# Turning the last weight in the first aggregation, and degree sums by way of VectorE, in a three-layer graph network on one core

## What is computed

```
deg     = segment_sum(1, dst);  deg_inv = 1 / max(deg, 1)
h       = relu(x @ W_self0 + (segment_sum(x[src], dst) * deg_inv) @ W_neigh0 + b0)
l0      =      h @ W_self1 + (segment_sum(h[src], dst) * deg_inv) @ W_neigh1 + b1
y       = layernorm(x + l0)
rows, cols = (src, dst) with every node's loop added
s       = (count of rows) ** -0.5
l1      = segment_sum(s[rows] * s[cols] * (y @ W.T + b)[cols], rows)
out     = layernorm(y + l1)
```

## Time and profile before

| | |
|---|---|
| median of three runs | 849.19 us |
| profiled execution | 849.59 us, span 847.9 |
| TensorE busy | 830.6 us |
| VectorE, ScalarE, POOL busy | 461.3, 177.4, 459.1 us |
| DMA | 180.52 MB, mean 213 GB/s |
| granted clock | 0.999 |

### The profile page before, as it was taken

One profiled execution on the slowest core, in us unless ns is written; L12 is line 12 of the kernel. 1 busy time (PEld: TensorE's weight loads), 2 busy tenths in 40 slices (PEclk: granted clock), 3 DMA queues, 4 the chain that ended last, 5 costly groups with the idle time before them and its releaser, 6 DMA issues.

```text
span 847.9 us, 11000 instructions
## 1 busy us (share of the span) xinstructions
PE 830.6 (98%) x4295; PEld 707.9 (83%) x4295; DVE 461.3 (54%) x714; ACT 177.4 (21%) x218; POOL 459.1 (54%) x343
## 2 busy tenths in 40 slices
PE   8999999999999999999999999999999999999996
PEld 6888888888897899788888888778889889988885
DVE  6465568200017565897544677775556435455555
ACT  4111132110111113353123112222222122200000
POOL 5028887787777887885888788788620000000000
PEclk9999999999999999999999999999999999999999
DMA  9977965463776425668876668267877649555551
GB/s 332 380 304 267 350 193 168 125 176 75 213 236 180 122 57 133 249 237 286 298 282 222 243 220 284 62 176 214 240 245 255 223 150 295 189 199 199 198 193 46
DMA packets 99480, 180.52 MB, mean 213 GB/s; under 512 B 15474, under 2 KB 75898, under 8 KB 94048
## 3 DMA queue, kind: packets, MB, share of 16 engines
q1 hardware_dynamic: 60144, 124.17, 44.0%
q10 hardware_dynamic: 26896, 40.65, 13.3%
q0 software_dynamic: 12384, 14.95, 7.6%
HBM read 107.08 MB, written 72.43 MB: 212 GB/s over the span
## 4 chain that ended last, share of the span: by engine, by line
PE 61%; POOL 15%; DMA 9%; issue 8%; DVE 5%; SPq 1%; ACT 1%; POOLq 0%; ACTq 0%; DVEq 0%
PE ps L1572 19%; POOL adj_in L643 14%; PE ps L1429 12%; PE ps L1606 10%; PE ps L1589 9%; PE ps L1515 8%; DMA adj_in<-u 4%; DMA first_rows<-in_L_gnn_W_neigh 1%; DMA spare<-in_x 1%; DMA xin<-s0t_scr 1%; PE ps L1413 1%; DVE u L914 1%; PE ps L1380 1%; SPq L514 1%; DVE sacc L1303 0%
## 5 line engine op out<-in xcount | busy, mean ns | idle before, releaser
L643 POOL DMA_INDIRECT adj_out<-loops,idx_out x160 | 245.2, 1533 | 65.4 <-issue 65.4
L643 POOL DMA_INDIRECT adj_in<-mult,idx_in x160 | 198.1, 1238 | 86.8 <-issue 86.8
L1572 PE MATMUL ps<-u 128*128 128x512 f32 x840 | 190.7, 389 | 1.4 <-DVE u L914 1.4
L1572 PEld LDWEIGHTS ps<-u 128*128 128x128 f32 x840 | 157.6, 188 | 34.2 <-issue 1.6
L1484 PE MATMUL ps<-wx 128*128 128x512 f32 (+1 forms) x576 | 109.4, 351 | 1.3 <-ACT outb L761 1.3
L1484 PEld LDWEIGHTS ps<-wx 128*128 128x128 f32 x576 | 93.9, 189 | 16.9 <-ACT outb L761 1.9
L1429 PE MATMUL ps<-u 128*128 128x512 f32 x432 | 98.2, 389 | 0.0
L1515 PE MATMUL ps<-wx,u 128*128 128x256 f32 (+5 forms) x640 | 94.8, 309 | 1.2 <-DVE ht L1191 1.2
L1589 PE MATMUL ps<-u,panel_tiles 128*128 128x512 f32 (+1 forms) x400 | 93.9, 393 | 1.9 <-DVE u L914 1.9
L1429 PEld LDWEIGHTS ps<-u 128*128 128x128 f32 x432 | 81.0, 188 | 16.8
L1515 PEld LDWEIGHTS ps<-wx,u 128*128 128x128 f32 (+1 forms) x640 | 86.6, 191 | 8.2 <-DVE ht L1191 1.6
(11 more groups left out here) (167 smaller groups left out, 779.8 us busy)
## 6 DMA issues: line engine op xcount, KB each, us to landing
left_scr<-u SPq DMA_DIRECT2D x7, 2560.0 KB, 9.5
u<-left_scr SPq DMA_DIRECT2D x7, 2560.0 KB, 9.6
xt_scr<-wx ACTq DMA_DIRECT2D x10, 1024.0 KB, 9.9
u<-xt_scr SPq DMA_DIRECT2D x10, 1024.0 KB, 5.1
wx<-xt_scr SPq DMA_DIRECT2D x16, 512.0 KB, 4.0
adj_in<-u POOLq DMA_DIRECT2D x4, 1600.0 KB, 25.3
adj_out<-u POOLq DMA_DIRECT2D x4, 1600.0 KB, 16.1
wx<-adj_in SPq DMA_DIRECT2D x5, 1280.0 KB, 7.1
```

Source lines behind the costliest of these rows:

```text
L643: pool.indirect_dma_start(table, bass.IndirectOffsetOnAxis(ap=index[0:EP, j:j + 1], axis=0), counts[0:EP, j:j + 1], None, bounds_check=CEL ...
L1572: ins = nc.tensor.matmul(ps[:, product_bank(g, i, p), :], left_op[n % 2][:, p, k, left, :], right_op[n % 2][:, k, right, :], start=(not on ...
```

## The change

The turning of the GCN weight moves from the second aggregation to the first: eight turns, behind blocks 3, 8, 12, 14, 17, 20, 23 and 26, each with its load (SP, ahead of the fetches of blocks 7, 12, 16, 18, 21, 24 and 27; the first at the end of stage 2) and its copy and store (ScalarE, behind the Relus of blocks 0, 5, 8, 10, 13, 16, 19 and 23). The degrees of chunks 0 and 1 are one matmul each with column sums made by VectorE, placed behind block 0 and behind block 11 (chunk 1, d=3). The one-column matmuls go; the reciprocals go through DRAM (`dinv_scr`) and come back as a column. The self parts of blocks 0 to 3 are fetched inside stage 2. The self stage has eight staging places. Some semaphores are merged.

```diff
+    TURN_BEHIND = {3: 0, 8: 1, 12: 2, 14: 3, 17: 4, 20: 5, 23: 6, 26: 7}
+    TURN_LOADS = {7: 1, 12: 2, 16: 3, 18: 4, 21: 5, 24: 6, 27: 7}
+    TURN_COPIES = {0: 0, 5: 1, 8: 2, 10: 3, 13: 4, 16: 5, 19: 6, 23: 7}
...
-        staged = [quarter(outb[:, :, :], j) for j in range(4)]
+        staged = [quarter(buf, j) for buf in (outb[:, :, :], raw[:, :, :]) for j in range(4)]
...
+            def fetch_self(m):
+                c, d = H_BLOCKS[m]
+                for i in [S0_BLOCKS.index((b, d)) for b in {0: (0,), 1: (0, 1), 2: (1,), 3: (2,)}[c]]:
+                    sp.wait_ge(s0_stored[i % 8], 16 * (i // 8 + 1))
+                if m >= 4:
+                    sp.wait_ge(h_sum, fetch_free(m))
+                sp.dma_start(fetch_slot(m)[:, 0:CHUNKS[c][1] * T], s0t_scr[d, :, lines(CHUNKS[c])]).then_inc(s0_in[m % 8], 16)
...
+                if i == 20:
+                    sp.wait_ge(xt_turned, NT)
+                    for m in range(4):
+                        fetch_self(m)
                 if i == 21:
                     load_chunk_1(0)
+            def load_turn(k):
+                if k == 0:
+                    sp.wait_ge(s0_full, 3 * KD)
+                else:
+                    sp.wait_ge(wt_turned, k)
+                sp.dma_start(turn_in[:, :], w_gcn[k * P:(k + 1) * P, :]).then_inc(wt_in, 16)
+
+            load_turn(0)
             sp.wait_ge(m1_full[0], 16)
             load_chunk_1(1)
...
             for m, (c, d) in enumerate(H_BLOCKS):
+                if m in TURN_LOADS:
+                    load_turn(TURN_LOADS[m])
                 if m >= 4:
+                    fetch_self(m)
                 if m in (15, 23):
                     load_chunk_1(2 + m // 17)
+                if d == 6:
+                    t0, n = CHUNKS[c]
+                    sp.wait_ge(dinv_row_done, c + 1)
+                    sp.dma_start(dinv_scr[lines(CHUNKS[c])].rearrange("(a j) -> a j", a=1), dinv_row[0:1, c % 2, 0:n * T]
+                                 ).then_inc(dinv_stored[c % 2], 16)
...
+            for s in range(2):
+                sp.wait_ge(dinv_stored[s], 16 * 2)
+            sp.dma_start(dinv[:, :], dinv_scr.rearrange("(t p) -> p t", p=P), allow_slow_non_contiguous=True).then_inc(dinv_in, 16)
...
+            def keep_turned(k):
+                act.wait_ge(wt_turned, k + 1)
+                if k > 0:
+                    act.wait_ge(wt_stored, 16 * k)
+                nc.scalar.activation(turn_out[:, :], pair_bank(3), ACT.Copy).then_inc(wt_copied, 1)
+                act.wait_ge(wt_copied, k + 1)
+                act.dma_start(wt_scr.rearrange("(k p) o -> p k o", p=P)[:, :, k * P:(k + 1) * P],
+                              turn_out.rearrange("p (k o) -> p k o", k=KD)).then_inc(wt_stored, 16)
...
                 if d == 0:
+                    if c < 2:
+                        dve.wait_ge(m1_full[c], 16 * n // 2)
+                        nc.vector.tensor_reduce(sacc[:, 0:width].rearrange("p (n j) -> p n j", n=n // 2),
+                                                m1_panels[c][:, :, :, :].bitcast(F32).rearrange("p k n j -> p n j k"), AX_X, ALU.add
+                                                ).then_inc(colsum_done, 1)
+                        dve.wait_ge(colsum_done, 2 * c + 1)
+                        nc.vector.tensor_copy(colsum[:, 0:width], sacc[:, 0:width]).then_inc(colsum_done, 1)
                     dve.wait_ge(deg_full, c + 1)
...
-                if d == 5:
-                    dve.wait_ge(dcol_full, c + 1)
-                    nc.vector.tensor_copy(dinv[:, t0:t0 + n], ps[:, 6 + c % 2, 0:n]).then_inc(dcol_read, 1)
...
+            def turn_weights(row, c):
+                pe.wait_ge(wt_in, 16 * (row + 1))
+                pe.wait_ge(deg_read, c + 1)
+                if row > 0:
+                    pe.wait_ge(wt_copied, row)
                 for k in range(KD):
+                    ins = nc.tensor.transpose(pair_bank(3)[:, k * P:(k + 1) * P], turn_in[:, k * P:(k + 1) * P], ident[:, :])
                 ins.then_inc(wt_turned, 1)
...
+            def degrees(c, width, exact):
+                pe.wait_ge(s0_free, s0_bank_free(6 + c))
+                if c == 1:
+                    pe.wait_ge(wt_copied, 2)
+                pe.wait_ge(colsum_done, 2 * c + 2)
...
+                    ins = nc.tensor.matmul(bank, ones_r[:, :], colsum[:, 0:width], start=True, stop=True)
+                ins.then_inc(deg_full, 1)
...
+                    if c >= 2:
+                        pe.wait_ge(deg_read, c - 1)
+                        pe.wait_ge(wt_copied, {2: 4, 3: 7}[c])
+                        for k in range(NT):
...
-                        if d == 2:
-                            pe.wait_ge(dinv_row_done, c + 1)
-                            for i in range(n):
-                                ins = nc.tensor.matmul(ps[:, 6 + c % 2, i:i + 1], dinv_row[0:1, c % 2, i * T:(i + 1) * T],
-                                                       ones_nt[0:1, 0:1], start=True, stop=True)
-                            ins.then_inc(dcol_full, 1)
+                        if (c, d) in ((0, 0), (1, 3)):
+                            degrees(c, width, exact)
+                        if m in TURN_BEHIND:
+                            turn_weights(TURN_BEHIND[m], 0 if m == 8 else c)
...
-                        if 1 <= t <= KD:
-                            turn_weights(t - 1)
```

More of the change, by code:

```diff
@@ L92, in build @@
         base = -(-nc.sbuf_base // 32) * 32
-        U_AT, WX_AT, R_AT, E_AT, END = (base + n for n in (0, 81920, 163840, 188416, 197120))
+        U_AT, WX_AT, R_AT, E_AT, B_AT, END = (base + n for n in (0, 81920, 163840, 188416, 197120, 201216))
         sb("arena", [P, (END - base) // 4], F32)
@@ L117, in build @@
         ones_r = sb("ones_r", [P, P], F32R)
-        bias = sb("bias", [P, D], F32)
+        bias = at("bias", [P, D], F32, B_AT)
+        colsum = at("colsum", [P, WIDE], F32R, B_AT)
         ident = sb("ident", [P, P], F32)
@@ L280, in build @@
         res_full = sems("res_full", 2)
-        wt_in = sems("wt_in", 2)
-        wt_stored = sems("wt_stored", 2)
+        wt_in = sem("wt_in")
+        wt_stored = sem("wt_stored")
         block_in = sems("block_in", 4)
@@ L318, in build @@
         s0_free = sem("s0_free")
+        colsum_done = sem("colsum_done")
         deg_full = sem("deg_full")
@@ L321, in build @@
         dinv_row_done = sem("dinv_row_done")
[L322 to L324 removed]
+        dinv_stored = sems("dinv_stored", 2)
+        dinv_in = sem("dinv_in")
         dsum_done = sem("dsum_done")
@@ L457, in load_chunk_1 @@
                     sp.wait_ge(h_full, KD * (c - 1))
-                    sp.wait_ge(dsum_done, sum(n for _, n in CHUNKS[:c - 1]) // 2)
+                    sp.wait_ge(dsum_done, sum(n for _, n in CHUNKS[:c - 1]))
                 for b in range(c + 1):
@@ L566, in _ @@
             sp.dma_start(bias[:, :], b_gcn.rearrange("(a d) -> a d", a=1).broadcast_to([P, D])).then_inc(bias_full, 16)
-            for s in range(2):
-                sp.wait_ge(wt_stored[s], 16 * KD // 2)
+            sp.wait_ge(wt_stored, 16 * KD)
             load_w(GCN, 0)
@@ L816, in _ @@
                 nc.scalar.activation(cell, cell, ACT.Relu).then_inc(h_done, 1)
+                if m in TURN_COPIES:
+                    keep_turned(TURN_COPIES[m])
                 if m == 27:
@@ L1265, in _ @@
                 u1_low(1, t0)
+            dve.wait_ge(dinv_in, 16)
             for t in range(NT):
@@ L1492, in typed @@
                 return ap.bitcast(F32) if exact else ap
+            def degrees(c, width, exact):
[3 more added lines that the diff above has]
+                pe.wait_ge(colsum_done, 2 * c + 2)
+                bank = ps[:, 6 + c % 2, 0:width]
+                if exact:
+                    ins = nc.tensor.matmul(bank, ones_r[:, :].bitcast(F32), sacc[:, 0:width], start=True, stop=True)
+                else:
+                    ins = nc.tensor.matmul(bank, ones_r[:, :], colsum[:, 0:width], start=True, stop=True)
+                ins.then_inc(deg_full, 1)
             def mean0(exact):
@@ L1498, in mean0 @@
                     pe.wait_ge(m1_full[c], 16 * n // 2)
-                    if c < 2:
-                        pe.wait_ge(s0_free, s0_bank_free(6 + c))
-                    else:
-                        pe.wait_ge(dcol_read, c - 1)
-                    for k in range(NT):
-                        ins = nc.tensor.matmul(ps[:, 6 + c % 2, 0:width].rearrange("p (n j) -> p n j", n=n // 2), typed(ones_r[0:rows(k), :], exact),
-                                               typed(panels[0:rows(k), k, :, :], exact), start=(k == 0), stop=(k == NT - 1))
-                    ins.then_inc(deg_full, 1)
+                    if c >= 2:
+                        pe.wait_ge(deg_read, c - 1)
+                        pe.wait_ge(wt_copied, {2: 4, 3: 7}[c])
+                        for k in range(NT):
+                            ins = nc.tensor.matmul(ps[:, 6 + c % 2, 0:width].rearrange("p (n j) -> p n j", n=n // 2),
```

(6 more changed lines are left out.)

79 lines of the change are left out of this document (27 added, 52 removed).

## The result

The changed kernel takes **856.12 us** (median of 5 runs, 855.13 to 858.18) against 849.65 (5 runs of the kernel before beside them, 848.74 to 851.98): a ratio of 1.0079, 95% interval 1.006 to 1.0097, so 0.8% slower. The profiled execution took 856.12, its span is 854.3 us, its mean granted clock 0.989. The forecast was 853.9 with a range of 845.5 to 859.0 and 0.50 on slower.

A forecast was written before the change was run, and what follows sets the result against it. TensorE, busy for 98% of the span, was taken as the bound. First aggregation +12.8 us and second -8.1 gave +4.7: 854.3 for the profiled execution, 853.9 against the median, range over the cases 845.5 to 859.0.

The forecast's parts named there:

- (A): First aggregation, chunk 0's degree sums: one matmul on VectorE's column sums replaces ten matmuls, -1.1 us.
- (B): First aggregation, chunk 1's degree sums: one 512-wide matmul is left and the wait on VectorE goes, -3.4 us.
- (C): First aggregation: the 20 one-column matmuls that turned the degrees go, -2.5 us.
- (D): Self stage, eight staging places: only a wait on a store leaves, between 0 and 1.3 us, taken as -0.3.
- (E): First aggregation: the eight turns come in at the same price, +7.0 us, between 6.3 and 8.3.
- (I): Second aggregation: shorter by 8.1 us, from eight turns (7.0) and a wait for ScalarE's copy (1.14).
- (F): First aggregation: chunk 3's degree matmuls wait for the copy of the turn directly ahead of them, +1.2 us.
- (G): First aggregation, behind block 14: TensorE waits for weight row 3, loaded late behind chunk 2's panel, +9.8 us (5.2 to 11.5).
- (H): First aggregation, behind the wait for row 3: the clock falls and matmuls run slowly, +2.1 us (0 to 4.2).
- the fourth row comes sooner: Rival, first aggregation: SP let go at 287.54, wait 4.1 to 5.2 us, clock holds; 846.1 or 847.2 us; chance 0.20.
- The scatter binds: Rival: no wait in the first aggregation, scatter bounds the GCN aggregation's panel; at most -5.7 us, 843.5; chance 0.08.
- The clock holds: Rival, first aggregation: clock kept through the wait for row 3; 851.8 us, no change by the bound; chance 0.13.

The follow-up runs named there:

- e12: e10 with the four early fetches of self parts issued behind the last load of the self stage instead of in it; 843.58 us, ratio 0.9931.
- e5: Changed kernel with the weight turned in the second aggregation as in the kernel before, the rest as changed; 849.18 us, ratio 0.9986.
- e6: e5 with the GCN weight not turned at all, so that part of the computation is left out; 844.71 us, ratio 0.9946.
- e3: Changed kernel with 44 matmuls of ones keeping TensorE busy ahead of the fourth turn; 852.17 us, ratio 1.0024.
- e1: Changed kernel with weight row 3 loaded ahead of the fetch for block 14 instead of 16, so ahead of chunk 2's panel; 850.97 us, ratio 1.0013.
- e2: Changed kernel with chunk 1's degrees by ten matmuls ahead of block 8, as in the kernel before; 849.60 us, ratio 0.9998.
- e8: e5 and the edit of e2 together: turning in the second aggregation, ten degree matmuls for chunk 1; 847.86 us, ratio 0.9974.
- e9: Changed kernel with row 3 and chunk 2's panel loaded sooner (at block 13's fetch), turns 1, 6 and 7 behind blocks 9, 24 and 27; 848.11 us, ratio 0.997.
- e11: e7 with turn 7 back behind block 26, its load at 26 and the copies at 20 and 23; 846.36 us, ratio 0.9964.
- e7: e2 with row 3 loaded at step 14, turns 1, 6 and 7 behind blocks 9, 24 and 27, copies at 21 and 26; 847.07 us, ratio 0.9961.
- e10: e9 with turn 7 back behind block 26, its load at 26 and the copies at 20 and 23; 844.97 us, ratio 0.9952.

## Why the prediction was right

The direction and the mechanism were right, and the size was 2.2 us short. By the steps of the prediction:

- **(A), (B), (C)**, the degree sums: right. Two single matmuls (0.28 and 0.40 us with drain), no one-column matmuls, no wait on VectorE between the chunks. Not forecast was that turn 1 would wait for its row, 0.78 us, though the crowding of SP's queue stood among the upper bounds as a reason for it. The column sums themselves were mis-sized without harm: VectorE came to chunk 1's at 264.5, not 260, and the reduce took 9.48 us, not 5.6, so that they were ready at 274.4, still ahead of the matmul.
- **(D)**, eight staging places: nothing gained (1.5 us waited, 1.3 before). The stage ended at 238.07, 1.0 later than in the sum. 0.67 of that is a wait in the kernel's first stage for ScalarE's split of a weight row (1.32 in e12, none before). It differs from run to run, and no edit touched it.
- **(E), (I)**, the turning: (I) is the best confirmed, -8.2 against -8.1 in the traces, -7.95 in e5 against e6. (E) is 0.80 to 0.85 of pace a turn, forecast at 0.87 (247.78 to 248.58, 263.76 to 264.61), 6.5 us for eight. So moving it wins little by itself, 1.7 us by these numbers and 1.1 by the forecast, and (F) takes 1.3 of it back.
- **(F)**, the copy ahead of chunk 3's degrees: 1.33, forecast 1.2.
- **(G)**, the late row: 10.70, forecast 9.8. Each event came 1.7 us later than worked out (block 11's sum 294.5 for 292.8), which is the late start and turn 1's wait carried through, and TensorE came 1.8 later too, so that cancels. The rest is SP's own steps (0.2) and the landing, 8.7 us after issue and not 7.9: row 3 came 1.9 us later behind the panel's issue than the small fetch did (9.1 for 7.2), for which the forecast had taken 1.1 and kept 1.9 as the bound. In e3 the same load took 7.7 us. That the order of the queue decides is shown by e1, that the late degree sums do by e2, and by e5 against e8.
- **(H)**, the clock: 0.8 on the turn and 1.8 on block 15, 2.65 by e3, forecast 2.1. This is a term that was mis-sized low. I had taken the loss of the kernel's first nine matmuls, 4.2 us of work; here the half clock went on for about 5.5 us of it.
- **The sum** of the first aggregation: forecast +12.8, measured +15.8 up to the products: late start 1.0, turn 1 0.8, G 0.9, H 0.6, F 0.1, which is 3.4, less 0.5 for (E). And 1.5 came back ahead of the second aggregation, a wait that the prediction took as unchanged (1.94 before, 0.84 at most in every run here, those with the turning in the second aggregation too); why it shrank wasn't traced. The late start and this gain stood in no term, and that they nearly cancel is luck.

The Trainium skill's rule that speaks here ("TensorE: Matmul & The Clock Gate", "HAM oscillation"), a wait for a DMA long enough to lower the clock makes the work behind it start at half rate, agrees with this trace (clock 0.50 in 300 to 308, and 2.65 us back in e3).

Of the **rivals**, "the fourth row comes sooner" is out by SP's rows (295.11, not 287.54). e2, where SP was let go at 288.05, has a wait of 2.91 and a lower clock behind it, so the rival's assumption that the clock holds for a wait of 4 to 5 us was wrong too. "The scatter binds" didn't come about, and its place was named wrong: e8 has it at chunk 3's panel, in the first aggregation, not at `adj_out`'s ahead of the GCN aggregation. Its bound of 629.6 there does not hold: in e6 POOL's last put is at 612.24, not 620.33, and the GCN aggregation begins at 628.86 without a wait. "The clock holds" is refuted by the stretches.

What the prediction missed, although it changed no number in it, is that the late panel of chunk 2 was a second wait under the first. I wrote its issue time (293.2) and not when TensorE wants it. Without the row's wait block 15 ends at 297.2 (291.7, a turn of 0.9, a block of 4.6), and the panel lands at 299.6 at the earliest (6.4 after its issue); so taking (G) away by the place of row 3's load alone brings a wait of 2.4 or more. e1 has 4.71, since the panel took 8.6 us (296.22 to 304.78). Its expectation had this wait, but at 2.5 us and with the clock kept.

## What to carry to other kernels

When a step is put behind another in a hand-written queue, write down for everything behind it the time at which it is wanted, not only for the step itself: here the wait for the weight row hid one for the panel, which was 4.7 us in e1, and removing the first alone won 5.2 us where a wait of 10.7 went. A sum that saves TensorE 2 us but lets VectorE begin a chunk 12 us later (278.90 for 267.10) isn't cheap, since VectorE's results free the slots by which the next transfers are let go. And when a stage is emptied, look for what fills the place: without its turns and without the late sums the first aggregation ran into the scatter (e8).

## What the hardware showed

- Short holes cost clock as well: after 2.91 us idle (e2) and 3.22 us (e8) the granted clock was at 0.50 for 2 us and more, and in e2 it fell only after work had begun again. The block behind e2's hole lost 1.6 us, more than half as much as the hole. The length of one hole doesn't tell: the clock also fell behind 2.05 us (e9) and, in the self stage of e5, e11 and e12, behind three waits of 0.3 to 0.6 us within 3 us of each other (1.6 us lost in each), but not behind 2.08 us (e1, at turn 1) or 2.33 us (e11, at the products), nor behind three such short waits in the changed kernel. What decides wasn't tested.
- VectorE's reduce with a stride: `128x5120` read across ten tiles took 9.48 us, where `128x2560` of neighbouring elements took 2.81; that is 1.85 ns an element against 1.10, 1.7 times as long. Chunk 0's, 2560 elements with the stride, took 4.83. The Trainium skill ("SBUF — State Buffer", "Specifications (TRN2)") says that every access which goes over to a new 16-byte line pays a penalty, and these reads, four bytes each with the tiles far apart, do so every time; the trace agrees, but the two reduces differ in more than the stride (sums of 10 elements against sums of 256) and no run varied it alone, so the cause isn't shown. With the degree matmul behind block 11 its length was hidden, as VectorE then waited 4.48 us anyway.
- A 512 KB load directly behind a 1280 KB panel on the same queue: it was there 8.7 us after its issue in the changed kernel, 10.1 in e2 and 7.7 in e3, where the earlier row of this kind of load had a median of 3.9.
- The medians of e7 to e11 lie 2.2 to 7.7 us above their expectations, and one kernel's runs spread over 3 to 9 us. Part of it is seen in single profiles, as waits of 0.3 to 2 us in the first stages and as the clock loss of the self stage, which other runs don't have; how often they come was not measured.
- Open: the 2.2 to 2.8 us ahead of the products in e10 to e12 (1.43 before); in e10 and e12 the clock fell to 0.50 behind them, in e11 it stayed at 1.00. A kernel without them wasn't tried.
